# The state-space stage of a decoder kernel: VectorE takes both channel halves in one product and one scan of 1024 columns

## The reference

```python
def _mamba_forward(x, ln_w, ln_b, W_in, conv_w, conv_b, W_xproj, W_dt, b_dt, A_log, D_param, W_out):
    xn = (x - mu) * lax.rsqrt(var + eps) * ln_w + ln_b
    x_in, z = jnp.split(xn @ W_in, 2, axis=-1)            # 256 channels each
    xc = _silu(causal_conv4(x_in, conv_w) + conv_b)
    dt_r, Bm, Cm = split(xc @ W_xproj)                    # 8, 16, 16
    dt = jax.nn.softplus(dt_r @ W_dt + b_dt)
    A = -jnp.exp(A_log)                                   # 256 channels x 16 states

    def step(h, inp):
        dt_t, B_t, C_t, u_t = inp
        dA = jnp.exp(dt_t[:, :, None] * A)
        h = h * dA + dt_t[:, :, None] * B_t[:, None, :] * u_t[:, :, None]
        y = jnp.einsum('bdn,bn->bd', h, C_t)
        return (h, y)
    y = scan(step) + xc * D_param
    return x + (y * _silu(z)) @ W_out
```

## Time and profile before

| What | Value |
|---|---|
| Median of 3 runs | 1927.17 us (1925.07 to 1928.24) |
| Span of the profiled execution | 1948.6 us; its time outside the span is not given |
| State-space stage in the trace | about 708 to 1290 us |
| VectorE over the span | 1491.3 us busy, 77% |
| TensorE over the span | 1562.9 us busy, 80% |
| GpSimd, ScalarE over the span | 920.7 us (47%), 953.5 us (49%) |
| Mean granted clock of TensorE | 0.916 |

### The profile page before, as it was taken

The page is one execution under the profiler, slowest core; times in us unless marked ns, Lnnn a source line. Parts: engine busy times, 40 slices in busy tenths (PEclk is TensorE's granted clock), DMA queues, the critical chain, the costliest instruction groups (busy, mean ns, idle before and its releaser), DMA issues. The chain is left out here.

```text
span 1948.6 us, 31799 instructions
## 1 busy us (share of the span) xinstructions
PE 1562.9 (80%) x10219; PEld 1017.4 (52%) x10219; DVE 1491.3 (77%) x2947; ACT 953.5 (49%) x1491; POOL 920.7 (47%) x938
## 2 busy tenths in 40 slices
PE   8889888989699978977878878769998811699991
PEld 4545547988476632322333333236776611588891
DVE  6899986887488779999989999967777678533335
ACT  3545543575544567657656666436566410011114
POOL 4455442444200147677676677654344100366653
PEclk8999998999899989999988999979999855799996
DMA  4000000000000000000000000020000040466654
GB/s 144 2 0 0 0 1 27 2 2 1 12 1 0 1 1 1 1 1 0 0 1 0 0 0 1 1 78 11 5 9 5 3 145 0 159 209 206 212 171 135
DMA packets 49075, 75.34 MB, mean 39 GB/s; under 512 B 8861, under 2 KB 34821, under 8 KB 48437
## 3 DMA queue, kind: packets, MB, share of 16 engines
q1 hardware_dynamic: 43541, 64.12, 10.5%
q0 software_dynamic: 4544, 9.32, 1.6%
q10 hardware_dynamic: 864, 0.33, 0.1%
HBM read 62.26 MB, written 11.48 MB: 38 GB/s over the span
## 5 line engine op out<-in xcount | busy, mean ns | idle before, releaser
L1506 POOL TENSOR_TENSOR m_hC<-m_h,m_Cs 128x512 f32<-128x512 f32 x256 | 328.2, 1287 | 169.2 <-DVE m_h L1680 122.6
L1788 PE MATMUL PS<-m_hC,identf 128*128 128x512 f32 x512 | 296.5, 662 | 100.9 <-POOL m_hC L1506 99.9
L1680 DVE TENSOR_TENSOR_SCAN m_h<-m_dA,PS 128x512 f32<-128x512 f32 x256 | 312.4, 1220 | 11.2
L1788 PEld LDWEIGHTS PS<-m_hC,identf 128*128 128x128 f32 x512 | 93.0, 203 | 236.4 <-POOL m_hC L1506 208.9
L1675 DVE TENSOR_TENSOR PS<-PS,m_DU 128x512 f32<-128x512 f32 x256 | 178.4, 697 | 19.9 <-issue 3.8
L1616 ACT ACTIVATE m_dA<-m_DT,m_A 128x508 f32<-128x508 f32 x256 | 174.3, 714 | 31.3 <-DVE m_DT L1664 31.1
L1996 ACT ACTIVATE e_Sg<-PS 128x512 f32<-128x512 f32 x71 | 42.4, 597 | 223.0 <-PE PS L2238 178.8
L2238 PE MATMUL PS<-e_xT,e_WT 128*128 128x128 f32 x1136 | 143.8, 281 | 4.9 <-DVE e_xT L2146 3.4
L1608 ACT COPY m_Cs<-PS 128x512 f32<-128x512 f32 x128 | 73.7, 576 | 143.7 <-PE PS L1766 143.5
L2238 PEld LDWEIGHTS PS<-e_xT,e_WT 128*128 128x128 f32 x1136 | 135.4, 195 | 9.3 <-DVE e_xT L2146 7.1
L1935 POOL DMA_INDIRECT e_XG<-token_rows,e_ids x71 | 68.8, 969 | 138.9 <-DVE e_ids L2140 117.6
(11 more groups left out here) (411 smaller groups left out, 3801.6 us busy)
## 6 DMA issues: line engine op xcount, KB each, us to landing
e_WT<-in_w_wgu SPq DMA_DIRECT2D x71, 512.0 KB
token_rows<-X SPq DMA_DIRECT2D x2, 2048.0 KB
e_Y<-expert_rows SPq DMA_DIRECT2D x16, 256.0 KB, 4.0
k_BD<-in_w_bcr SPq DMA_DIRECT2D x1, 2464.0 KB, 9.5
e_w_wd<-in_w_wd SPq DMA_DIRECT2D x1, 2048.0 KB, 7.9
out_dram<-X SPq DMA_DIRECT2D x8, 256.0 KB, 2.4
X<-in_x SPq DMA_DIRECT2D x1, 1792.0 KB, 8.7
x_Cs<-in_ctx SPq DMA_DIRECT2D x8, 154.0 KB
```

The costliest lines, as they stand in the source:

```text
L1506: nc.gpsimd.tensor_tensor(hC[:, i % ND, :], hst[:, i % ND, :], Cs[:, n % ND, :], ALU.mult).then_inc(s["hC"], 1)
L1680: nc.vector.tensor_tensor_scan(hst[:, i % ND, :], dA[:, i % NA].rearrange("p b l -> p (b l)"), bank(4), 0.0, ALU.mult, ALU.add).then_inc(s ...
L1788: nc.tensor.matmul(bank(5 + ch), c.identf[:, :], hC[:, i % ND, :], start=False, stop=(n == NS - 1)).then_inc(s["yacc"], 1)
```

## The change

VectorE issues for each state (even i) one product and one scan over both halves, 1024 columns each, and nothing at odd i. The product goes into banks 3 and 4 (BU); its B operand is read twice by a stride of zero. B has one bank (1), C has bank 2. The semaphores h and dBu count states, no longer steps: GpSimd's hC of both halves waits for the joined scan, ScalarE's dA for the scan of state n - 4, VectorE's first product of a group for both halves of DU, its scan for both dA and for the hC of the state two before. TensorE sends B(n+2) at the even step, ahead of C(n+1), and waits there for product n+1. The number of the other instructions, and all SLOT numbers, stay.

```diff
--- before.py
+++ after.py
@@ -1428,6 +1428,7 @@
     Cs = sb("Cs", [P, ND, T])
     hC = sb("hC", [P, ND, T])
     ln, iln = c.ln, {k: (c.sb("m_i" + k, v.shape, F32, ctx) if k not in ("half", "eps") else v) for k, v in c.ln.items()}
+    BB, BC, BU = 1, 2, 3
     bank = lambda i, r=P: PS[0:r, i, :]
     bl = lambda ap: ap.rearrange("p (b l) -> p b l", b=GB)
     SLOT = {"last_c": 0, "gate": 1, "output0": 1, "silu_z": 3, "output1": 3, "rstd": 6, "stats": 6, "norm": 11, "x0": 8, "x1": 9, "x2": 11, "inner_stats": 11,
@@ -1499,7 +1500,7 @@
 
             def step(g, par, i, left):
                 n = i // CH
-                pool.wait_ge(s["h"], g * NI + i + 1)
+                pool.wait_ge(s["h"], g * NS + n + 1)
                 pool.wait_ge(s["Cs"], g * NS + n + 1)
                 if not first(g, i, ND):
                     pool.wait_ge(s["yacc"], g * NI + i - ND + 1)
@@ -1605,14 +1606,14 @@
                 act.wait_ge(s["C"], g * NS + n + 1)
                 if not first(g, n, ND):
                     act.wait_ge(s["hC"], g * NI + CH * (n - ND + 1))
-                nc.scalar.copy(Cs[:, n % ND, :], bank(3)).then_inc(s["Cs"], 1)
+                nc.scalar.copy(Cs[:, n % ND, :], bank(BC)).then_inc(s["Cs"], 1)
 
             def step(g, par, i, left):
                 n, ch = i // CH, i % CH
                 if i < CH:
                     act.wait_ge(s["dt"], g * CH + i + 1)
                 if not first(g, i, NA):
-                    act.wait_ge(s["h"], g * NI + i - NA + 1)
+                    act.wait_ge(s["h"], g * NS + n - NA // CH + 1)
                 nc.scalar.activation(dA[:, i % NA, :, 1:P], bl(DT[:, par, ch, :])[:, :, 1:P], ACT.Exp, scale=A[:, ch, n:n + 1]).then_inc(s["dA"], 1)
                 if ch == 1 and n >= LAG:
                     c_copy(g, n - LAG)
@@ -1665,19 +1666,23 @@
                 return stage
 
             def step(g, par, i, left):
+
                 n, ch = i // CH, i % CH
-                if i < CH:
-                    dve.wait_ge(s["du"], g * CH + i + 1)
-                if ch == 0:
-                    dve.wait_ge(s["B"], g * NS + n + 1)
-                if not first(g, i, 1):
-                    dve.wait_ge(s["h"], g * NI + i)
-                nc.vector.tensor_tensor(bank(4), bank(1 + n % 2), DU[:, par, ch, :], ALU.mult).then_inc(s["dBu"], 1)
-                dve.wait_ge(s["dBu"], g * NI + i + 1)
-                dve.wait_ge(s["dA"], g * NI + i + 1)
+                if ch:
+                    return
+                pair = slice(i % ND, i % ND + CH)
+                if n == 0:
+                    dve.wait_ge(s["du"], g * CH + CH)
+                dve.wait_ge(s["B"], g * NS + n + 1)
+                if not first(g, n, 1):
+                    dve.wait_ge(s["h"], g * NS + n)
+                nc.vector.tensor_tensor(PS[:, BU:BU + CH, :], bank(BB).rearrange("p (o t) -> p o t", o=1).to_broadcast([P, CH, T]), DU[:, par], ALU.mult).then_inc(s["dBu"], 1)
+                dve.wait_ge(s["dBu"], g * NS + n + 1)
+                dve.wait_ge(s["dA"], g * NI + i + CH)
                 if not first(g, i, ND):
-                    dve.wait_ge(s["hC"], g * NI + i - ND + 1)
-                nc.vector.tensor_tensor_scan(hst[:, i % ND, :], dA[:, i % NA].rearrange("p b l -> p (b l)"), bank(4), 0.0, ALU.mult, ALU.add).then_inc(s["h"], 1)
+                    dve.wait_ge(s["hC"], g * NI + i + CH - ND)
+                nc.vector.tensor_tensor_scan(hst[:, pair, :].rearrange("p c t -> p (c t)"), dA[:, i % NA:i % NA + CH].rearrange("p c b l -> p (c b l)"),
+                                             PS[:, BU:BU + CH, :].rearrange("p c t -> p (c t)"), 0.0, ALU.mult, ALU.add).then_inc(s["h"], 1)
 
             def gate(g, par):
                 dve.wait_ge(s["yacc"], g * NI + NI)
@@ -1754,16 +1759,16 @@
             def spread_b(g, par, n):
                 if n == 0:
                     pe.wait_ge(s["lo"], g + 1)
-                if not first(g, n, 2):
-                    pe.wait_ge(s["dBu"], g * NI + CH * (n - 1))
-                nc.tensor.matmul(bank(1 + n % 2), W["sel"][:, n:n + 1].to_broadcast([96, P]), hi[:, par, :], start=True, stop=True).then_inc(s["B"], 1)
+                if not first(g, n, 1):
+                    pe.wait_ge(s["dBu"], g * NS + n)
+                nc.tensor.matmul(bank(BB), W["sel"][:, n:n + 1].to_broadcast([96, P]), hi[:, par, :], start=True, stop=True).then_inc(s["B"], 1)
 
             def spread_c(g, par, n):
                 if n == 0:
                     pe.wait_ge(s["lo"], g + 1)
                 if not first(g, n, 1):
                     pe.wait_ge(s["Cs"], g * NS + n)
-                nc.tensor.matmul(bank(3), W["sel"][:, NS + n:NS + n + 1].to_broadcast([96, P]), hi[:, par, :], start=True, stop=True).then_inc(s["C"], 1)
+                nc.tensor.matmul(bank(BC), W["sel"][:, NS + n:NS + n + 1].to_broadcast([96, P]), hi[:, par, :], start=True, stop=True).then_inc(s["C"], 1)
 
             def step(g, par, i, left):
                 n, ch = i // CH, i % CH
@@ -1772,14 +1777,14 @@
                     spread_c(0, 0, 0)
                     spread_b(0, 0, 1)
                 if ch == 0:
+                    if n + 2 < NS:
+                        spread_b(g, par, n + 2)
+                    elif left:
+                        spread_b(g + 1, 1 - par, n + 2 - NS)
                     if n + 1 < NS:
                         spread_c(g, par, n + 1)
                     elif left:
                         spread_c(g + 1, 1 - par, 0)
-                elif n + 2 < NS:
-                    spread_b(g, par, n + 2)
-                elif left:
-                    spread_b(g + 1, 1 - par, n + 2 - NS)
                 if n == 0:
                     if not (isinstance(g, int) and g == 0):
                         pe.wait_ge(s["y1"], g * 2 - 1 + ch)
```

## The result

| | Median, us | Runs |
|---|---|---|
| Before | 1927.25 (1925.07 to 1928.71) | 7 |
| Changed | 1933.48 (1932.72 to 1934.34) | 7 |
| Ratio | 1.0032, 95% interval 1.0023 to 1.0041 | |

What follows compares the result with a forecast made beforehand. The prediction took VectorE's own stream to set the stage's pace. Savings of 51.2 (pairs) and 8.1 (old gate waits), less 40.3 (new waits), 1.25 (end) and 1.35 (start), gave 16.4 us less: 1910.8 us, range 1888 to 1933.

Steps and rivals of the forecast that it cites:

- Joined pair: One state's product and scan on VectorE: 3.64 us, 0.40 less than before, 51 us over 128 pairs.
- Each microsecond it saves counts one for one until another engine is late: Claim that VectorE's own stream sets the stage's pace, so the pairs' 51.2 us saving counts in full.
- the ring: Later theory, not forecast: gate, TensorE to x3, ScalarE to logarithms, GpSimd corrections, softplus, two pairs, DU(1), product 0, accumulations, gate.
- the four waits: Added VectorE waits per group: dA at scan 9 1.5, softplus0 2.6, DU(1) 1.35, gate 0.3; together 5.75 us.
- Softplus: VectorE's wait at softplus0, slot 27, for GpSimd's corrections: 2.6 us per group, ends 1.4 and 4.
- Gate: VectorE's wait before the gate, after pair 0's scan: 0.3 us per group, while the old 8.1 us go.
- B: Product waits on B's spread from one bank: costed at nothing, TensorE about 1.7 us late at B(3), 1.9 allowed.
- rival C: TensorE at half clock makes x3 and everything behind 5 us later per group: 35 us lost, 1946; chance 0.18.
- The later dt1, mids and low: ScalarE and TensorE work in pairs 9 to 11, costed at nothing; without cover 0.6 to 1.1 us each per group.
- The gap of 0.03 us between product and scan: VectorE's idle time inside each joined pair, taken as 0.03 us of the pair's 3.64.
- Rival A: Added waits mostly hidden by engines catching up in plain pairs' slack: 2 us per group left, 1885; chance 0.16.
- Rival B: Nothing left: the scan saves nothing or waits are 8 us instead of 5.75; 1927 to 1933, chance 0.12.

Runs made afterwards that it cites:

- e7: Changed kernel with VectorE's wait for its product put between the waits for dA and hC: 1933.62 us, ratio 1.0029 to the kernel before.
- e8: Changed kernel with the edits of e5 and e7 together: 1920.50 us, ratio 0.9972 to the kernel before.
- e13: a1 plus one unused GpSimd product per group between the first and second correction: 1927.26 us, ratio 1.0003 to the kernel before.
- e14: a1 plus one unused GpSimd product per group in a plain pair, ahead of hC(12): 1917.84 us, ratio 0.9955 to the kernel before.
- e5: Changed kernel plus seven zero-adding TensorE matmuls per group around the softplus and DU waits: 1921.78 us, ratio 0.9965 to the kernel before.
- a0: Changed kernel itself run again, nothing edited: 1935.52 us, ratio 1.0030 to the kernel before.
- e12: a1 plus three more zero-adding matmuls per group, at steps 3, 4 and 5: 1913.79 us, ratio 0.9934 to the kernel before.
- a1: e9 run once more, as the base for e12, e13 and e14: 1920.36 us, ratio 0.9964 to the kernel before.
- e9: Changed kernel with e5's matmuls, and C(n+1) sent at the even step, B(n+2) at the odd: 1918.30 us, ratio 0.9947 to the kernel before.
- e2: Changed kernel with TensorE sending C(n+1) at the even step and B(n+2) at the odd one: 1956.14 us, ratio 1.0014 to the kernel before.
- e6: Kernel before with one bank for B and the changed order of spreads, nothing joined: 2003.63 us, ratio 1.0394 to the kernel before.

## Why the prediction was wrong, by its steps

1. **The sizes were right.** Joined pair: product 1.229 for 1.225, scan 2.287 for 2.27. Over the stage VectorE is busy 40.8 us less with them (256 x 1.917 = 490.8, 128 x 3.516 = 450.0); the forecast had 128 x 0.34 = 43.
2. **"Each microsecond it saves counts one for one until another engine is late" failed.** It was read from VectorE's 64 of 70 busy us. In the changed kernel that is 59.84, and the time is set by the ring. e7 and e8 took time off the plain pairs and gained nothing that can be told from noise; e13 and e14 show one link that counts. The limit stood in the trace before: from x3 to the logarithms it has the same 20.7 us, and softplus0 began 0.4 us (mean) after it could have. The forecast did count the four waits on that ring, but then added the saving of all 128 pairs to them as if the two could be booked apart. The waits are what is left of a ring longer than VectorE's stream: shorten the pairs and they grow. With the matmuls of e5 in both kernels the join is worth 4 to 7 us, not 16.4.
3. **The four waits.** Softplus 18.4 for 18.2, DU 12.1 for 10.8 (1.55 us each for 1.35), dA 9.9 for 10.5, though in 17 waits and not in one per group. Gate: 6.8 for 2.1, up to 2.0 us where it waits, for 0.3, because TensorE did the last two accumulations at half clock. B: 14.1 for 0; the forecast had TensorE 1.7 us late at B(3), of 1.9 allowed, and at full clock; e5 brings it to 5.3.
4. **The price of rival C stood outside the sum.** The mechanism was named and even placed ("waits 2 and 3 leave TensorE idle longer, just ahead of the output stages"), then given 0.18 because the mean clock was 0.98 in the earlier trace rows. That window of before has no softplus wait in it; a wait that the change adds can't be read from it. The runs give its size: e5 takes 69 (against after) or 84 us (against a0) of half clock away and the time falls 12 to 14 us; e12 takes a further 24 away against a1 and 6.6 us go. Of the miss of 22.6 us some 10 to 13 go with the clock: the join costs 0.0030 without the matmuls and gains 0.0020 (e5) to 0.0038 (e9, which has C first besides) where both kernels have them. The rest is step 2. That e12, with the clock held and C first, comes out at 1913.8, 3 us from the forecast, is luck: the forecast had neither. C's 1946 was too dear, as the low clock costs about 2 us a group (13.7 over 7), not 5. The low clock did come in every group: each of the seven softplus waits is followed by a window at 0.80 or less, and those from 785, 920, 935, 1070, 1085 and 1165 us are at 0.50. This agrees with the rule of the Trainium skill, "TensorE: Matmul & The Clock Gate", Part 1, that idling brings the low clock. It reached the gate in four groups of seven; in the other three the gate did not wait.
5. **"The later dt1, mids and low, which lie in ScalarE's and TensorE's free time of pairs 9 to 11" failed in its reason.** From 910 to 915 us ScalarE works 4.92 of 5 us up to the logarithms that softplus waits for, and in the trace before it was no freer (4.97 of 5 from 905 to 910). Of each softplus wait 1.3 us are GpSimd's alone (e12, where GpSimd waits for the logarithms only once, 0.5 us), near the 1.4 forecast; the other 1.0 to 1.9 come from C's copy and the logarithms behind it. e2 shows that link: C's copy earlier, softplus wait 10.3 for 18.4, though B waits gave most of it back.
6. **The gap of 0.03 us between product and scan** was taken over from the earlier trace rows; in the loop it is 0.19. It is 0.16 x 96 = 15 us of VectorE's time. e7 and e8 took about 11 of them away and gained nothing clear: a wrong term that hardly mattered, as most of these pairs are off the ring.

Rival A's premise, slack elsewhere that hides the waits, was wrong, as GpSimd's slack lies in plain pairs, while the four corrections run back to back. Rival B's time, 1927 to 1933, was right and its causes were not: the scan saves 0.15 us a pair, and the four waits came to 6.7 us a group, not 8.

## What to carry to other kernels

A busy share of 90% doesn't say that an engine's instructions are all on the path: follow one period from an event to its next occurrence through all engines, and test a link by putting a dummy operation on it and the same one beside it, and by taking time off what should lie beside it. Where a change adds waits to one engine, write down how long TensorE stands still for each, and work out the time also with the matmuls behind it at half clock; a few matmuls that add zero can be cheaper than the clock that they hold.

## What the runs showed that was not expected

- A register operation that waits for the product puts 0.19 us between product and dependent scan. With the wait on an instruction of its own it is 0.09 (e7: 967.79 - 966.47 - 1.23), in the groups with constants too. With the wait on the scan itself it is 0.03 before and 0.04 in the changed kernel's groups with constants (1255.89 - 1254.62 - 1.23).
- Seven matmuls a group that add nothing, 0.86 us each, made a kernel whose TensorE is 80% busy faster by 14 us.
- Idle time of VectorE at the turn of a loop is 0.3, 1.9 or 4.0 us in programs that differ in their VectorE instructions; the cause is open.
- One bank for B, with B sent ahead of C and without the joined product, costs 75 us (e6).
